# QKV product of a windowed attention kernel: two halves of 288 columns instead of 192 and 384, and the transposed v written beside the forward transform

## The chip, the cores and the metric

The kernel runs on one core of one Trainium2 chip. The metric is the device time of one execution in microseconds (us); lower is better. TensorE (PE) multiplies and loads weights, VectorE (DVE), ScalarE (ACT) and GpSimd (POOL) work element by element, and SyncE (SP) issues the DMAs.

## The reference

The input `x` has shape 8 x 192 x 128 x 128 in float32. Layer 0 normalises groups of channels, makes q, k and v with a 1x1 convolution, and works on windows of 8 x 8 tokens with 6 heads of 32 channels. The product of the Fourier transforms of q and k replaces q times k, and its inverse is the "o" that meets v:

```
qkv3 = wins.reshape(B_, N, 3, NH, HD).transpose(2, 0, 3, 1, 4)
o = jnp.fft.irfft2(jnp.fft.rfft2(qp) * jnp.fft.rfft2(kp), s=(PS, PS))
attn = jnp.einsum('bhnd,bhmd->bhnm', o, vv) + bias[None]
attn = jax.nn.softmax(attn, axis=-1)
y = jnp.einsum('bhnm,bhmd->bhnd', attn, vv)
x = x + (1x1 convolution of y)
```

Layer 1 normalises again, adds a Laplacian stencil and applies a 1x1 convolution (the "merge").

## The kernel before

A strip of 8 image rows holds 16 windows, so 8 pairs of windows (128 tokens each); there are 128 strips and 1024 pairs. The code is unrolled over iterations `it`. Each engine's instructions are written out by hand in one order, and `pair(lag)` is the pair on which an iteration works `lag` steps late. Eight iterations make a block; here "pair 0" to "pair 7" are the places in a block. Layer 1 follows 18 blocks behind: from then on iterations 0 to 5 of each block also hold a "piece", one 256-column part of the merge product. So the program has a head (statistics, tables), a first stage of 18 blocks without pieces, a second stage of 110 blocks with them, and a tail in which only pieces are left.

TensorE does in an iteration, in this order: transposes of the probabilities of pair n-4 (L418), a piece (L394 to L401), q, k and v of pair n (L456), two transposes of v (L460), the output projection of pair n-5 (L472 to L475), y of pair n-4 (L485), the inverse transform o of pair n-1 (L495), the forward transform of pair n (L505) and the scores of pair n-1 (L525). The QKV product is five products of split operands (high and low parts), accumulated. V's 192 columns go first, into their own bank, then Q's and K's 384 columns into the other bank of `b_q`.

The other engines follow on semaphores. ACT copies v out (`vs`, which raises `v_out`), takes the exponential of pair n-2 (L904), rounds q and k (`qkh`), copies the transposed v (`vT`, which raises `vT_out`), then y (`yT`), o (`osb`) and the transform of q (`qh`). All of these copies have line L859. DVE adds the position bias to the scores (L712), takes their maximum (L717), multiplies the transforms (`prod`, L721, which raises `prod_done`), does the stencil and statistics, then the remainder of q and k (`qkl`, L800, which raises `lo_out`), the residual (L808) and the sums (L818). POOL subtracts the maximum (L947), normalises (L936), and once in four pairs makes `xl` (L942). ACT also splits the input, once in four pairs, in three copies (`xhl`, `xh`, `xhb`) that stand just ahead of `vs` in its queue.

Three waits matter. The transposes wait for `v_out`; the QKV product waits for `vT_out` of the pair before; the forward transform waits for `lo_out`. The forward transform writes 384 of the 512 columns of each of the two banks of `b_t`, and DVE reads them for `prod` in the next iteration.

Of the kernel before, what the change touches and what calls it, by code (L numbers as in the profile page):

```python
# [13 lines left out]
C = 192  # L14
# [3 lines left out]
QK, QKV = 2 * C, 3 * C  # L18
# [72 lines left out]
def program(nc, x, out, w):  # L91
# [13 lines left out]
    with ExitStack() as ctx:  # L105
# [6 lines left out]
        def sem(name):  # L112
# [21 lines left out]
        vs, vT = sb("vs", [128, 5, C]), sb("vT", [128, 2, 2, 128])  # L134
# [26 lines left out]
        mw1, mb2 = late[0:2, at + 16:at + 16 + HID], late[0:1, at + 16 + HID:at + 16 + HID + N * NH]  # L161

        b_q, b_t, b_o, b_s = ps("b_q", 2), ps("b_t", 2), ps("b_o", 1), ps("b_s", 3)
        q_out, v_psum, vt_out = b_q[:, 0:QK], b_q[:, 512:512 + C], b_q[:, 512 + C:512 + C + 256]
        m_out = b_o[:, 192:512]
        b_r, scores, b_p = b_s[:, 0:256], b_s[:, 512 - C:512 + C], b_s[:, 1024:1024 + NH * N]
        y_at = (512 + C, 1024 + NH * N)
# [13 lines left out]
        v_mm, qkv_mm, t_mm, vT_mm, s_mm, pT_mm, y_mm, proj_mm, o_mm = map(sem, (  # L181
            "v_mm", "qkv_mm", "t_mm", "vT_mm", "s_mm", "pT_mm", "y_mm", "proj_mm", "o_mm"))
        lo_out, prod_done, s_out, max_done, sum_done, rec_done, x1_done = map(sem, (
            "lo_out", "prod_done", "s_out", "max_done", "sum_done", "rec_done", "x1_done"))
# [148 lines left out]
        def _(pe):  # L333
# [77 lines left out]
            for it, pair in pairs():  # L411
# [31 lines left out]
                if pair(0):  # L443
                    i, n = pair(0)
                    h, par = i // 4, i // NP % 2
                    if pair(1):
                        pe.wait_ge(vT_out, n - 1)
                    at = slice(i % 4 * 128, i % 4 * 128 + 128)
                    products = [(xh, wnh, 0), (xh, wnl, 0), (xhb, wnh, 1), (xl, wnh, 0), (xhl, wnl, 1)]
                    if i % 4 == 0:  # L450
                        pe.wait_ge(xh_done, 3 * (h + 1))
                        pe.wait_ge(xl_done, h + 1)
                        pe.wait_ge(xhl_done, h + 1)
                    for o, lo, up, done in ((v_psum, QK, QKV, v_mm), (q_out, 0, QK, qkv_mm)):
                        for k, (xx, ww, t) in enumerate(products):
                            last = mm(o, xx[:, h % 2, at], ww[:, par, t, lo:up], start=(k == 0), stop=(k == 4))  # L456
                        last.then_inc(done, 1)
                    pe.wait_ge(v_out, n)
                    for t in range(2):
                        last = nc.tensor.transpose(vt_out[:, t * 128:(t + 1) * 128],  # L460
                                                   vs[:, i % 5, t * N:t * N + 128], ident[:, :])
                    last.then_inc(vT_mm, 1)
                if pair(5):
# [35 lines left out]
                if pair(0):  # L499
                    i, n = pair(0)  # L500
                    pe.wait_ge(lo_out, n)
                    for k, (ff, xx) in enumerate(((fwdh, qkh), (fwdh, qkl), (fwdl, qkh))):
                        for win in range(2):
                            rows = slice(win * N, (win + 1) * N)
                            last = mm(b_t[0:NF, win * 512:win * 512 + QK], ff[rows, :], xx[rows, :],  # L505
                                      start=(k == 0), stop=(k == 2))
                    last.then_inc(t_mm, 1)
# [346 lines left out]
        def _(act):  # L854
# [3 lines left out]
            def copy(o, i):  # L858
                return A.activation(o, i, ACT.Copy)  # L859
# [15 lines left out]
            for it, pair in pairs():  # L875
# [29 lines left out]
                if pair(0):  # L905
                    i, n = pair(0)
                    act.wait_ge(qkv_mm, n)
                    copy(qkh[:, :], q_out).then_inc(hi_out, 1)
                    act.wait_ge(vT_mm, n)
                    copy(vT[:, i % 2, :, :].rearrange("p t m -> p (t m)"), vt_out).then_inc(vT_out, 1)  # L910
                if pair(4):
                    i, n = pair(4)
                    act.wait_ge(y_mm, n)
# [66 lines left out]
```

## Time and profile before

| | us |
|---|---|
| median of 3 runs | 6623.4 (6617.2 to 6633.11) |
| the profiled execution, its own time | 6616.41 |
| its span, first to last instruction | 6614.6 |
| PE busy, share of the span | 95% |
| DVE busy | 80% |
| ACT busy | 55% |
| POOL busy | 31% |
| mean granted TensorE clock | 0.978 of full speed |

Busy shares of TensorE count pipelined matmuls whose ends are modelled; the distance from one start to the next says more than the length of a row. An idle time in brackets stands in front of the instruction that ended it, with the instruction that released it.

### The profile page before, as it was taken

Reading aid. Unit: us, or ns where it says so; the run is one execution under the profiler, and the core shown is the slowest. Engines: PE = TensorE matmul, PEld = TensorE weight load, DVE = VectorE, ACT = ScalarE, POOL = GpSimd, SP = SyncE. Lnnn points to the kernel's source line nnn. Section 1 sums busy time; section 2 is a strip of 40 time slices with the busy share of each in tenths; the row PEclk is TensorE's granted clock in tenths of the full one; section 3 lists DMA queues with packets and bytes.
Section 4 is the critical chain, followed back from the end, with each engine's and each line's share of the span. In section 5 each row is a group of like instructions: output and inputs, shape, how many; then the busy total and the mean of one; then the engine's idle time right before and its main releaser. Section 6 shows DMA issues by size and latency. Waiting matters only on the chain.

```text
span 6614.6 us, 222120 instructions
## 1 busy us (share of the span) xinstructions
PE 6291.9 (95%) x95620; PEld 5340.6 (81%) x95620; DVE 5312.2 (80%) x11941; ACT 3664.4 (55%) x9024; POOL 2064.8 (31%) x2310
## 2 busy tenths in 40 slices
PE   7999999999999999999999999999999999999976
PEld 5888788888888888888888888888888888888844
DVE  5777788888888888888888888888888888888854
ACT  3666655555555555555555555555555555555500
POOL 1333333333333333333333333333333333333300
PEclk9999999999999999999999999999999999999966
DMA  3221133232332322322333223323223222232233
GB/s 128 66 66 40 56 93 90 84 84 82 89 104 71 97 82 83 104 70 81 98 90 96 72 82 92 101 77 91 82 83 104 77 78 70 64 85 64 69 99 92
DMA packets 378995, 551.42 MB, mean 83 GB/s; under 512 B 23398, under 2 KB 283561, under 8 KB 365738
## 3 DMA queue, kind: packets, MB, share of 16 engines
q1 hardware_dynamic: 378028, 537.21, 28.5%
q8 instruction: 768, 12.58, 0.8%
q14 instruction: 199, 1.63, 0.1%
HBM read 335.80 MB, written 201.33 MB: 81 GB/s over the span
## 4 chain that ended last, share of the span: by engine, by line
PE 58%; DVE 25%; POOL 9%; ACT 6%; issue 2%; SPq 0%; DMA 0%; DVEq 0%; ACTq 0%
PE b_q L456 13%; PE b_t L505 7%; POOL probs L947 5%; PE b_s L525 5%; PE b_s L418 4%; DVE qkl L800 4%; DVE bn L705 4%; PE b_o L495 4%; PE b_o L394 3%; DVE late L808 3%; PE b_o L396 3%; ACT probs L904 3%; DVE ssum L818 3%; PE b_s L485 3%; POOL xl L942 3%; DVE probs L712 2%
## 5 line engine op out<-in xcount | busy, mean ns | idle before, releaser
L936 POOL TENSOR_TENSOR probs<-probs,srec 128x384 f32<-128x384 f32 x1024 | 849.3, 829 | 3723.1 <-DVE srec L851 3723.1
L800 DVE TENSOR_TENSOR qkl<-b_q,qkh 128x384 fp32r<-128x384 f32 x1024 | 567.6, 554 | 634.9 <-ACT qkh L859 628.3
L947 POOL TENSOR_TENSOR probs<-probs,smax 128x384 f32<-128x384 f32 x1024 | 908.0, 887 | 413.8 <-DVE smax L717 413.8
L712 DVE TENSOR_TENSOR probs<-b_s,posb 128x384 f32<-128x384 f32 x1024 | 553.0, 540 | 331.2 <-PE b_s L525 330.6
L904 ACT ACTIVATE probs<-probs 128x384 f32<-128x384 f32 x1024 | 535.3, 523 | 479.8 <-POOL probs L947 479.1
L456 PE MATMUL b_q<-wnh,xh 128*128 128x192 f32 (+1 forms) x2048 | 791.7, 387 | 3.1 <-DVE xhl L822 2.7
L859 ACT ACTIVATE probsT<-b_s 128x384 f32<-128x384 f32 x1024 | 502.4, 491 | 501.3 <-PE b_s L418 501.3
L859 ACT ACTIVATE qh<-b_t 94x384 f32<-94x384 f32 x1024 | 498.4, 487 | 480.4 <-PE b_t L505 480.4
L525 PEld LDWEIGHTS b_s<-vT,osb 32*64 32x64 f32 x24576 | 450.6, 132 | 284.5 <-ACT osb L859 204.9
L859 ACT ACTIVATE yT<-b_s 128x256 f32<-128x256 f32 x1024 | 392.7, 384 | 460.3 <-PE b_s L485 458.2
L456 PE MATMUL b_q<-wnl,xh 128*128 128x192 f32 (+1 forms) x2048 | 632.5, 309 | 0.0
L808 DVE SCALAR_TENSOR_TENSOR late<-b_s,pb,xs 128x128 f32<-128x128 f32 (+1 forms) x2048 | 610.1, 339 | 27.2 <-PE b_s L475 5.2
L456 PE MATMUL b_q<-wnl,xhl 128*128 128x192 f32 (+1 forms) x2048 | 631.0, 308 | 0.0
L456 PE MATMUL b_q<-wnh,xhb 128*128 128x192 f32 (+1 forms) x2048 | 630.5, 308 | 0.0
L456 PE MATMUL b_q<-wnh,xl 128*128 128x192 f32 (+1 forms) x2048 | 629.6, 307 | 0.0
L859 ACT ACTIVATE vs<-b_q 128x192 f32<-128x192 f32 x1024 | 334.9, 327 | 518.6 <-PE b_q L456 512.9
L717 DVE TENSOR_REDUCE smax<-probs 128x6 f32<-128x384 f32 x1024 | 566.5, 553 | 35.5
L525 PE MATMUL b_s<-vT,osb 32*64 32x64 f32 x24576 | 592.4, 225 | 0.9 <-DVE late L808 0.7
L505 PE MATMUL b_t<-qkh,fwdh 64*94 64x384 f32 x2048 | 423.1, 410 | 171.0 <-DVE qkl L800 170.7
L495 PE MATMUL b_o<-inv_sb,prod 94*64 94x64 f32 x12288 | 582.9, 230 | 0.0
L418 PE MATMUL b_s<-ident_sb,probs 128*128 128x128 f32 x3072 | 561.3, 292 | 1.2 <-ACT yT L859 1.2
L721 DVE TENSOR_TENSOR prod<-qh,b_t 94x384 f32<-94x384 f32 x1024 | 553.5, 541 | 1.9 <-ACT qh L859 1.9
(143 smaller groups left out, 15231.2 us busy)
## 6 DMA issues: line engine op xcount, KB each, us to landing
ld<-in_x SPq DMA_DIRECT2D x96, 1024.0 KB, 4.9
late<-x_dram SPq DMA_DIRECT2D x112, 640.0 KB, 6.3
xs<-in_x SPq DMA_DIRECT2D x128, 512.0 KB, 5.7
x_dram<-late SPq DMA_DIRECT2D x128, 512.0 KB, 2.8
out<-late SPq DMA_DIRECT2D x128, 512.0 KB, 4.6
late<-x_dram SPq DMA_DIRECT2D x240, 192.0 KB, 6.7
xs<-in_x SPq DMA_DIRECT2D x128, 256.0 KB, 6.3
x_dram<-late SPq DMA_DIRECT2D x128, 256.0 KB, 3.6
```

The source lines that it names most:

```text
L418: last = nc.tensor.transpose(b_p[:, t * 128:(t + 1) * 128], probs[:, i % 3, 2 * t:2 * t + 2, :].rearrange("p w m -> p (w m)"), ident[:, :])
L456: last = mm(o, xx[:, h % 2, at], ww[:, par, t, lo:up], start=(k == 0), stop=(k == 4))
L495: last = mm(b_o[g * N:(g + 1) * N, k * N:(k + 1) * N], prod[:, g * 3 + k, :, :].rearrange("p h d -> p (h d)"), inv[:, :], start=True, stop ...
L505: last = mm(b_t[0:NF, win * 512:win * 512 + QK], ff[rows, :], xx[rows, :], start=(k == 0), stop=(k == 2))
L525: last = mm(scores[h * N:(h + 1) * N, s * N:(s + 1) * N], osb[r:r + HD, k, :], vT[r:r + HD, i % 2, int(t > g), win * N:(win + 1) * N], sta ...
L712: V.tensor_tensor(scored(i).rearrange("p (t w) m -> p t w m", w=2), scores.rearrange("p (t w m) -> p t w m", w=2, m=N), posb[:, :, :].unsq ...
L800: V.tensor_tensor(qkl[:, :], q_out, qkh[:, :].bitcast(F32), ALU.subtract).then_inc(lo_out, 1)
L808: last = V.scalar_tensor_tensor(out=x1s[0:m, t, u % 2, :].rearrange("p (r c) -> p r c", c=W)[:, :, col:col + 16], in0=b_r[0:m, t * 128:(t ...
L859: return A.activation(o, i, ACT.Copy)
L904: A.activation(pr, pr, ACT.Exp).then_inc(exp_done, 1)
L936: P.tensor_tensor(probs[:, i % 3, :, :], probs[:, i % 3, :, :], srec[:, i % 2, :].unsqueeze(2).broadcast_to([128, 6, N]), ALU.mult).then_i ...
L947: P.tensor_tensor(probs[:, i % 3, :, :], probs[:, i % 3, :, :], smax[:, i % 2, :].unsqueeze(2).broadcast_to([128, 6, N]), ALU.subtract).th ...
```

## The change

The ten matmuls of QKV stay ten, with 2880 columns in sum, but are cut at column 288 instead of 384. The half with the last 96 columns of K and all of V goes first and fills bank 1 of `b_q` from its start; the half with Q and the first 96 columns of K goes second and fills bank 0 up to its end. So Q and K still lie side by side, now across the banks' border. The transposed v is written to the last 128 columns of each bank of `b_t`. Two waits follow from this, and one goes.

```diff
-        q_out, v_psum, vt_out = b_q[:, 0:QK], b_q[:, 512:512 + C], b_q[:, 512 + C:512 + C + 256]
+        first = 512 - QKV // 2
+        q_out, v_psum = b_q[:, first:first + QK], b_q[:, first + QK:first + QKV]
+        vt_out = b_t.rearrange("p (t c) -> p t c", t=2)[:, :, QK:512]
...
-                    if pair(1):
-                        pe.wait_ge(vT_out, n - 1)
...
-                    for o, lo, up, done in ((v_psum, QK, QKV, v_mm), (q_out, 0, QK, qkv_mm)):
+                    for lo, up, done in ((QKV // 2, QKV, v_mm), (0, QKV // 2, qkv_mm)):
+                        o = b_q[:, first + lo:first + up]
...
                     pe.wait_ge(v_out, n)
+                    if pair(1):
+                        pe.wait_ge(prod_done, n - 1)
                     for t in range(2):
-                        last = nc.tensor.transpose(vt_out[:, t * 128:(t + 1) * 128],
+                        last = nc.tensor.transpose(vt_out[:, t, :],
...
                     pe.wait_ge(lo_out, n)
+                    pe.wait_ge(vT_out, n)
...
-                    copy(vT[:, i % 2, :, :].rearrange("p t m -> p (t m)"), vt_out).then_inc(vT_out, 1)
+                    copy(vT[:, i % 2, :, :], vt_out).then_inc(vT_out, 1)
```

The order of the instructions on TensorE at the start of a pair without a piece, before the change (`wnh`, `wnl` are the weights' high and low parts, `xh`, `xl`, `xhb`, `xhl` those of the input):

```order
L456 MATMUL b_q<-wnh,xh 128x192 [waits vT_out]
L456 MATMUL b_q<-wnl,xh 128x192
L456 MATMUL b_q<-wnh,xhb 128x192
L456 MATMUL b_q<-wnh,xl 128x192
L456 MATMUL b_q<-wnl,xhl 128x192
L456 MATMUL b_q<-wnh,xh 128x384
L456 MATMUL b_q<-wnl,xh 128x384
```

The same place on TensorE in the changed kernel:

```order
L457 MATMUL b_q<-wnh,xh 128x288
L457 MATMUL b_q<-wnl,xh 128x288
L457 MATMUL b_q<-wnh,xhb 128x288
L457 MATMUL b_q<-wnh,xl 128x288
L457 MATMUL b_q<-wnl,xhl 128x288
```

The five rows then come a second time for the other half. No instruction is added or taken away; the widths change and the first wait is gone.

From the transposes of v to the forward transform, TensorE before the change:

```order
L460 MATMUL b_q<-ident_sb,vs 128x128 [waits v_out]
L460 MATMUL b_q<-ident_sb,vs 128x128
L472 MATMUL b_s<-yT,wp 128x128 [waits s_out]
L473 MATMUL b_s<-yT,wp 128x128
L474 MATMUL b_s<-yT,wp 128x128
L475 MATMUL b_s<-yT,wp 128x128
L485 MATMUL b_s<-probsT,vs 32x64 [waits s_out,pT_out]
L485 MATMUL b_s<-probsT,vs 32x64 x11
L495 MATMUL b_o<-inv_sb,prod 64x64 [waits prod_done]
L495 MATMUL b_o<-inv_sb,prod 64x64 x5
L505 MATMUL b_t<-qkh,fwdh 94x384 [waits lo_out]
```

The same place in the changed kernel:

```order
L463 MATMUL b_t<-ident_sb,vs 128x128 [waits prod_done,v_out]
L463 MATMUL b_t<-ident_sb,vs 128x128
L475 MATMUL b_s<-yT,wp 128x128 [waits s_out]
L476 MATMUL b_s<-yT,wp 128x128
L477 MATMUL b_s<-yT,wp 128x128
L478 MATMUL b_s<-yT,wp 128x128
L488 MATMUL b_s<-probsT,vs 32x64 [waits s_out,pT_out]
L488 MATMUL b_s<-probsT,vs 32x64 x11
L498 MATMUL b_o<-inv_sb,prod 64x64 [waits prod_done]
L498 MATMUL b_o<-inv_sb,prod 64x64 x5
L509 MATMUL b_t<-qkh,fwdh 94x384 [waits vT_out,lo_out]
```

The wait for `prod_done` of the pair before has moved ahead of the projection and y, and the forward transform waits for two semaphores.

## Rows read from the trace of the kernel before

**Rows 1.** The page, busy time by engine.

```profile
PE 6291.9 (95%) x95620; PEld 5340.6 (81%) x95620; DVE 5312.2 (80%) x11941; ACT 3664.4 (55%) x9024; POOL 2064.8 (31%) x2310
```

**Rows 2.** Waits of TensorE (us in total, times, longest), second stage (902:6290).

```profile
PE b_t L505 <- DVE qkl L800: 133.7, 211, 1.6
```

**Rows 3.** Timeline (start us, us) of TensorE, pair 3 of one second-stage block.

```profile
2045.97 0.44 PE L456 MATMUL b_q<-wnh,xh 128*128 128x192 f32 x1
2046.25 0.28 PE L456 MATMUL b_q<-wnl,xh 128*128 128x192 f32 x1
...
2046.59 0.27 PE L456 MATMUL b_q<-wnl,xhl 128*128 128x192 f32 x1
2046.70 0.36 PE L456 MATMUL b_q<-wnh,xh 128*128 128x384 f32 x1
...
2047.42 0.34 PE L456 MATMUL b_q<-wnl,xhl 128*128 128x384 f32 x1
2047.59 0.38 PE L460 MATMUL b_q<-ident_sb,vs 128*128 128x128 f32 x2
...
2049.65 0.41 PE L505 MATMUL b_t<-qkh,fwdh 64*94 64x384 f32 x2
```

**Rows 4.** Timeline of DVE in the same pair.

```profile
2046.11 0.54 DVE L721 TENSOR_TENSOR prod<-qh,b_t 94x384 f32<-94x384 f32 x1
...
2048.31 0.56 DVE L800 TENSOR_TENSOR qkl<-b_q,qkh 128x384 fp32r<-128x384 f32 x1 [0.66 <-ACT qkh L859]
```

**Rows 5.** Timeline of TensorE where its granted clock is 0.5.

```profile
1626.61 0.41 PE L456 MATMUL b_q<-wnl,xh 128*128 128x192 f32 x1
...
1627.46 0.57 PE L456 MATMUL b_q<-wnh,xh 128*128 128x384 f32 x1
1627.84 0.52 PE L456 MATMUL b_q<-wnl,xh 128*128 128x384 f32 x1
...
1628.80 0.52 PE L456 MATMUL b_q<-wnl,xhl 128*128 128x384 f32 x1
```

**Rows 6.** Timeline of TensorE, the two instructions of one 288-column bias product.

```profile
745.00 0.51 PE L372 MATMUL b_o<-wn,negmean 128*128 128x288 f32 x1
...
745.34 0.41 PE L372 MATMUL b_o<-wn,negmean 128*128 128x288 f32 x1
```

**Rows 7.** Timeline of ACT in the pair of rows 3.

```profile
2046.90 0.33 ACT L859 ACTIVATE vs<-b_q 128x192 f32<-128x192 f32 x1 [0.91 <-PE b_q L456]
```

**Rows 8.** Timeline of TensorE and DVE, pair 0 of the same block.

```profile
2029.02 0.54 DVE L721 TENSOR_TENSOR prod<-qh,b_t 94x384 f32<-94x384 f32 x1
...
2029.27 0.38 PE L460 MATMUL b_q<-ident_sb,vs 128*128 128x128 f32 x2
...
2031.22 0.53 DVE L800 TENSOR_TENSOR qkl<-b_q,qkh 128x384 fp32r<-128x384 f32 x1
...
2031.81 0.41 PE L505 MATMUL b_t<-qkh,fwdh 64*94 64x384 f32 x2 [0.41 <-DVE qkl L800]
```

**Rows 9.** Timeline of DVE and TensorE, pair 7 of the same block.

```profile
2070.98 0.54 DVE L721 TENSOR_TENSOR prod<-qh,b_t 94x384 f32<-94x384 f32 x1
...
2071.46 0.38 PE L460 MATMUL b_q<-ident_sb,vs 128*128 128x128 f32 x2
```

**Rows 10.** Waits of the weight loader, first stage (98:902).

```profile
PEld b_q L460 <- ACT vs L859: 15.2, 68, 1.1
```

**Rows 11.** Timeline of TensorE and DVE, pair 0 of a first-stage block.

```profile
447.12 0.38 PE L460 MATMUL b_q<-ident_sb,vs 128*128 128x128 f32 x2
...
447.20 0.54 DVE L721 TENSOR_TENSOR prod<-qh,b_t 94x384 f32<-94x384 f32 x1
...
449.77 0.41 PE L505 MATMUL b_t<-qkh,fwdh 64*94 64x384 f32 x2 [0.53 <-DVE qkl L800]
```

**Rows 12.** Timeline of DVE and TensorE at the first pair, where three semaphores are waited for.

```profile
97.33 0.69 DVE L822 TENSOR_TENSOR xhl<-xs,xhl 64x512 fp32r<-64x512 f32 x1
...
98.16 0.50 PE L456 MATMUL b_q<-wnh,xh 128*128 128x192 f32 x1 [2.72 <-DVE xhl L822]
```

## The prediction

> **What bounds the kernel now.** I read the page first: TensorE is busy for 95% of the span, the weight loader for 81%, DVE for 80% [rows 1]. That says who is nearest to full, not who ends a wait, so the waits of the second stage come next, since it holds 880 of the 1024 pairs (110 blocks of eight). There the forward transform waits for `qkl` in 211 pairs, 133.7 us in sum [rows 2], about two pairs in a block. The timelines show which. In pair 0 TensorE stands still for 0.41 us before the forward transform, which starts 0.06 us after the end of `qkl` (2031.22 + 0.53 = 2031.75) [rows 8]; pair 6 is the other. In pair 3, `qkl` ends at 2048.87 and the forward transform starts at 2049.65 [rows 3, 4]: DVE is 0.78 us early and TensorE sets the time. So pairs 1 to 5 are TensorE's, and what it saves there shortens the kernel; in pairs 0, 6 and 7 a chain through DVE, POOL and ACT sets it, and a saving of TensorE turns into waiting.
>
> That gives a count. 880 less 211 are 669 pairs without the wait. One in each block, pair 7, I take off: its `prod` ends at 2070.98 + 0.54 = 2071.52, later than its transposes start (2071.46) [rows 9], and the change makes them wait for it. Left are 559, five in a block.
>
> **The ten matmuls.** In pair 3 the first matmul of V starts at 2045.97 and the second at 2046.25; that first step belongs to the piece ahead and stays. From 2046.25 the starts are (2046.70 - 2046.25) / 4 = 0.1125 us apart with 192 columns. From 2046.70 to the transposes at 2047.59 are 0.89 us for five of 384 columns, 0.173 each and some 0.02 on the first. Together 1.34 us from the second matmul to the transposes [rows 3].
>
> Now per column: 384 columns at 2.4 per ns are 0.160, so 0.173 is the stream and 0.013 more. But 192 columns would be 0.080 and take 0.1125. Something else bounds them. The stretch at half clock (granted 0.5, the 1.2 GHz level) says what: (1627.46 - 1626.61) / 4 = 0.2125 with 192 columns, (1628.80 - 1627.84) / 3 = 0.320 with 384 [rows 5]. 0.320 is 384 columns at 1.2 per ns exactly; 0.2125 is what 255 columns would take, and so is 0.1125 at full clock but for 5 ns. So a 192-column matmul costs as much as 256, a floor that I put down to the load of 128 fp32 weights under it. Half of V's issue is empty. With 288 columns the stream is above the floor.
>
> The price of 288 columns isn't in the trace for this form. Nearest is the bias product: its two instructions pass 288 columns twice each, and end at 745.51 and 745.75 [rows 6], 0.24 us for 576 columns, 0.120 for 288. From below that is 0.120, nothing on top. From the row of 384, with the same 0.013 on top, it is 0.133. A straight line between 0.1125 and 0.173 gives 0.143. At worst it costs what 384 do, 0.173, if widths were rounded up. Rows 6 exclude rounding for the bias form, so I take 0.133: nine steps and 0.02 are 1.22 us instead of 1.34, a saving of 0.12 a pair.
>
> TensorE: Matmul & The Clock Gate, section Back-to-back issue gap, in the Trainium skill, gives a spacing of N/2.4 + 2.5 ns at full clock, which is 0.1225 us for 288 columns (an estimate from that page). The trace disagrees at both widths that it has (0.083 against 0.1125, 0.1625 against 0.173), so the sum doesn't use it; with it the matmuls alone would save 1.34 - 1.12 = 0.22 a pair.
>
> **The copy of v.** It can start only when the first half is done, and that is now 96 columns longer. Before, the copy starts at 2046.90, 0.04 after V's last matmul ends (2046.59 + 0.27), and ends at 2047.23; the transposes' weights are loaded from about 2047.42 [rows 3, 7]. After: V's half has its last start at 2046.25 + 3 x 0.133 = 2046.65; it lasts some 0.31 (between 0.27 and 0.34), so the copy runs from 2047.00 to 2047.33, and the load may begin 0.05 to 0.10 later, at 2047.38 to 2047.43. Unhindered it would begin at about 2047.34. So the wait for `v_out`, which has 0.19 us to spare now, is at its edge. The load has some slack against the stream before it; I take 0.01 as lost, 0.11 as the saving. This also caps it: at 0.120 a matmul the copy ends only at 2047.29, so no more than some 0.18 to 0.20 can be won in a pair.
>
> 559 x 0.11 = 61 us.
>
> **The wait for `prod_done` ahead of the transposes.** The transposes now go to the banks that `prod` is read from. Behind them on TensorE are projection, y, o and the forward transform; ACT waits for y and o. In pair 3 `prod` ends at 2046.65, 0.94 before the transposes [rows 3, 4]: free. In pair 0 it ends at 2029.56, and they start at 2029.27 [rows 8]. The hold-up is 0.29, about 0.06 for the release, and some 0.05 because their weights can't be loaded ahead: 0.40. This goes into the 0.41 of idle time before the forward transform in the same pair, since `qkl` is set by a chain that doesn't contain the transposes. Cost nothing, with nothing to spare. In pair 7 the hold-up is 0.16; the next forward transform that matters, pair 0's, is set by DVE, which is busy without a break from pair 7 into pair 0, so it is hidden too. In the first stage pair 0 (and pair 4 alike) has `prod` ending at 447.74 against a start of 447.12 [rows 11]: 0.62 + 0.11 = 0.73 held up, and 0.53 of idle time, which by the starts of o and the transform is nearer 0.58. So 0.15 is lost twice a block, 18 x 2 x 0.15 = 5 us. The same stage gains nothing, for in half its pairs the transposes already wait for `vs` (68 of 144 [rows 10]), held by a copy of the input ahead of it on ACT, and in others the wait for `qkl` ends last.
>
> **Two waits on one instruction.** Where the trace has one wait before a matmul it starts 0.06 after the release [rows 8]; with three it starts 0.14 after (97.33 + 0.69 = 98.02, start 98.16) [rows 12]. So a second wait costs between 0 and 0.08 where the semaphore that comes last is checked first; `lo_out` is written first. I take 0.05, in pair 0 of 110 blocks (in pair 6 DVE hides it) and in some three pairs of the 18 first blocks: 8 us. The wait for `vT_out` itself is free: the copy `vT` ends before `qkl` does. The dropped wait cost nothing, and copies, bytes and DMAs stay as they are.
>
> **Sum.** -61 + 5 + 8 = -48 us, so 6616.4 becomes 6568. The median of the runs shown is 7 us above the profiled time, hence 6575.
>
> **The rivals.**
> *The copy's cap is reached.* 288 columns at 0.120 to 0.1225: 0.19 x 559 = 106 saved, less 13: -93, 6530. For it: the bias rows. Against: no fp32r row of full clock runs without the extra. 0.12.
> *Interpolated price, 0.143.* The pair saves 1.34 - 1.31 = 0.03: -17 + 13 = -4 us, 6619, no change. For it: if the floor of the weight load and the stream add up partly. 0.11.
> *Rounded up: 288 cost what 384 do.* 9 x 0.173 + 0.02 = 1.58, 0.24 more in 559 pairs: +134, with the 13 above and some 20 in the first stage near 6790. Against it are rows 6 and the linear 0.320. It decides from 0.146 a matmul. 0.06.
> *The hold-ups aren't hidden.* If `qkl` or POOL's and ACT's chain moves with the held transposes, 0.40 + 0.16 a block in 110 blocks and 0.73 twice in 18 are 62 + 26 = 88 instead of 5: +35 us, 6658, slower. Point of decision: more than about 0.45 of the 0.56 per block showing. For it: ACT copies y and o, both now late, ahead of the next block's work; against: `qh` follows the forward transform, later still. 0.08.
>
> **How the numbers follow.** My forecast, a gain of 20 to 75 us with 0.11 a pair as its middle, has 0.63. A measurement of this kernel tells from no change about 0.2%, 13 us. Faster by more: 0.63 + 0.12 and 0.01 of the interpolated case, 0.76; within: 0.10; slower: 0.06 + 0.08 = 0.14. The range takes in the first rival and the interpolated price, and leaves out the slower cases: 6528 to 6620.
>
> **What would show it.** Pair 3 after: starts of the ten matmuls 0.133 apart (0.120, 0.143 or 0.173 name the rival), transposes 0.11 to 0.12 earlier after the second matmul, `vs` starting 0.10 later. Block length in the second stage shorter by 0.5 to 0.55 us. Pair 0: transposes some 0.05 after `prod`, idle time before the forward transform near 0, its start still 0.06 to 0.11 after `qkl`. Waits of the forward transform for `qkl` fewer or shorter; first stage longer by 5 to 10 us. The prediction is wrong if the price of 288 is off by more than 0.01, or if pairs 1 to 5 begin to wait for `vs` or `qkl`.

## The result and the profile after

| kernel | median us | lowest to highest | runs |
|---|---|---|---|
| before | 6626.27 | 6617.2 to 6633.11 | 4 |
| after | 6564.04 | 6561.89 to 6579.31 | 4 |

The ratio is 0.9912, its 95% interval 0.9895 to 0.9928: the change makes the kernel 58 us faster, by its middle. The profiled execution took 6561.89 us. The page of the kernel after, its head and the busy times, answers to [rows 1]:

```profile
span 6560.1 us, 223912 instructions
PE 6223.4 (95%) x95620; PEld 5256.2 (80%) x95620; DVE 5294.0 (81%) x11941; ACT 3630.8 (55%) x9024; POOL 2064.4 (31%) x2310
```

TensorE is as full as before, on a span 54.5 us shorter than the 6614.6 of before. Where that came from is read by stage. I cut the span at the starts of the first QKV matmul of pair 0, of pair 144 (where the pieces begin) and of the last pair. Windows of the kernel after, then the second stage of the kernel before; behind the stretch stand its length, the five busy times with their counts, the granted clock, the DMA share and GB/s:

```profile
98.00:906.90 808.90, 755.68 (x12682) 627.14 (x12683) 581.08 (x1353) 498.76 (x1257) 285.51 (x319) 1.00 0.19 57
906.90:6234.90 5328.00, 5171.34 (x81574) 4441.75 (x81572) 4491.10 (x10147) 3106.99 (x7725) 1771.13 (x1977) 1.00 0.30 85
6234.90:6560.00 325.10, 230.85 (x803) 145.54 (x801) 176.27 (x355) 9.35 (x21) 5.80 (x7) 0.66 0.35 95
```

```profile
904.10:6289.70 5385.60, 5232.48 (x81574) 4512.28 (x81572) 4509.87 (x10148) 3146.29 (x7724) 1771.56 (x1977) 1.00 0.30 84
```

The second stage went from 5385.6 to 5328.0 us, 57.6 less; the first from 805.9 to 808.9, 3.0 more; head and tail are as before. So all of the gain is in the second stage. Its pairs, as the median distance from one pair's first QKV matmul to the next pair's:

| pair of a block | 0 | 1 | 2 | 3 | 4 | 5 | 6 | 7 |
|---|---|---|---|---|---|---|---|---|
| before, us | 6.438 | 5.957 | 5.957 | 6.375 | 6.375 | 5.176 | 6.050 | 5.872 |
| after, us | 6.236 | 5.840 | 5.844 | 6.259 | 6.277 | 5.082 | 6.040 | 6.075 |

Pairs 1 to 5 each gained 0.09 to 0.12, 0.54 in all, and 0.54 x 110 blocks is 59 us. Pair 7 lost 0.20 and pair 0 won the same 0.20 back. This is the pattern to explain; pair 3 after on TensorE, to be laid beside [rows 3] (start, duration):

```profile
2036.34 0.48 PE L457 MATMUL b_q<-wnh,xh 128*128 128x288 f32 x1
2036.66 0.30 PE L457 MATMUL b_q<-wnl,xh 128*128 128x288 f32 x1
2036.80 0.29 PE L457 MATMUL b_q<-wnh,xhb 128*128 128x288 f32 x1
...
2037.72 0.29 PE L457 MATMUL b_q<-wnl,xhl 128*128 128x288 f32 x1
2037.85 0.38 PE L463 MATMUL b_t<-ident_sb,vs 128*128 128x128 f32 x2
2039.91 0.41 PE L509 MATMUL b_t<-qkh,fwdh 64*94 64x384 f32 x2
```

From the second matmul to the transposes are 1.19 us in nine steps, 0.132 each, where 1.34 were needed. The first step became longer, 0.32 instead of 0.28. Together the ten take 1.51 us where they took 1.62. ACT's copy of v in the same pair, which answers to [rows 7]:

```profile
2037.39 0.33 ACT L863 ACTIVATE vs<-b_q 128x192 f32<-128x192 f32 x1 [1.03 <-PE b_q L457]
```

It ends at 2037.72, 0.13 before the transposes start. Before, it ended 0.36 ahead of them. Now pair 0, TensorE and then DVE, beside [rows 8]:

```profile
2018.44 0.48 PE L457 MATMUL b_q<-wnh,xh 128*128 128x288 f32 x1
...
2019.82 0.29 PE L457 MATMUL b_q<-wnl,xhl 128*128 128x288 f32 x1
2020.32 0.41 PE L463 MATMUL b_t<-ident_sb,vs 128*128 128x128 f32 x2 [0.20 <-DVE prod L725]
...
2022.42 0.41 PE L509 MATMUL b_t<-qkh,fwdh 64*94 64x384 f32 x2
```

```profile
2019.63 0.54 DVE L725 TENSOR_TENSOR prod<-qh,b_t 94x384 f32<-94x384 f32 x1
...
2021.83 0.53 DVE L804 TENSOR_TENSOR qkl<-b_q,qkh 128x384 fp32r<-128x384 f32 x1
```

`prod` ends at 2020.17 and the transposes start 0.15 later. Pair 7 of the same block, beside [rows 9], shows the same distance (2061.03 + 0.54 = 2061.57, start 2061.72):

```profile
2061.72 0.41 PE L463 MATMUL b_t<-ident_sb,vs 128*128 128x128 f32 x2 [0.16 <-DVE prod L725]
```

```profile
2061.03 0.54 DVE L725 TENSOR_TENSOR prod<-qh,b_t 94x384 f32<-94x384 f32 x1
```

In pairs 1 to 5 the transposes start 0.13 after the last QKV matmul started; in pair 0 it is 0.49 and in pair 7 0.45 (medians of the stage). So they are held up by 0.36 and 0.32, which is about what these two pairs have to give: 0.11 each, saved by the matmuls, and the 0.41 of idle time in front of pair 0's forward transform. That still starts 0.06 after `qkl` (2022.36), now without idle time before it. The waits of TensorE say the same for all blocks of the second stage (total us, times, longest), beside [rows 2]:

```profile
PE b_t L509 <- DVE qkl L804: 99.5, 128, 1.7
PE b_t L463 <- DVE prod L725: 33.0, 165, 0.8
```

The forward transform waits in 128 pairs for 99.5 us instead of in 211 for 133.7, and a new wait of 33.0 us stands at the transposes. The sum has hardly moved.

### The profile page after: what moved, and what is told of

It reads as the page before. It is cut to its first block, busy times and chain, and to the rows that moved or that the text cites. A ratio compares the mean times of both kernels' runs of the same rounds, so it can differ in the third digit from the quotient of the medians.

```text
span 6560.1 us, 223912 instructions
## 1 busy us (share of the span) xinstructions
PE 6223.4 (95%) x95620; PEld 5256.2 (80%) x95620; DVE 5294.0 (81%) x11941; ACT 3630.8 (55%) x9024; POOL 2064.4 (31%) x2310
## 4 chain that ended last, share of the span: by engine, by line
PE 61%; DVE 23%; POOL 9%; ACT 5%; issue 2%; SPq 0%; DMA 0%; DVEq 0%; ACTq 0%
PE b_q L457 12%; PE b_t L509 7%; PE b_s L529 5%; POOL probs L951 5%; PE b_o L498 4%; PE b_s L420 4%; DVE bn L709 4%; PE b_s L488 3%; PE b_o L396 3%; DVE late L812 3%; PE b_o L398 3%; DVE qkl L804 3%; DVE ssum L822 3%; PE b_t L463 3%; POOL xl L946 3%; ACT probs L908 2%
## 5 line engine op out<-in xcount | busy, mean ns | idle before, releaser
L457 PE MATMUL b_q<-wnh,xh 128*128 128x288 f32 x2048 | 762.2, 372 | 2.8 <-DVE xhl L826 2.7
L457 PE MATMUL b_q<-wnh,xl 128*128 128x288 f32 x2048 | 606.8, 296 | 0.0
L457 PE MATMUL b_q<-wnl,xhl 128*128 128x288 f32 x2048 | 606.0, 296 | 0.0
L457 PE MATMUL b_q<-wnh,xhb 128*128 128x288 f32 x2048 | 605.6, 296 | 0.0
L457 PE MATMUL b_q<-wnl,xh 128*128 128x288 f32 x2048 | 605.5, 296 | 0.0
L822 DVE TENSOR_REDUCE ssum<-probs 128x6 f32<-128x384 f32 x1024 | 546.2, 533 | 0.0
```

Source lines behind the costliest of these rows:

```text
L822: V.tensor_reduce(ssum[:, i % 2, :], scored(i), AX.X, ALU.add).then_inc(sum_done, 1)
```

## The experiments

Eleven more runs follow, one of them of the kernel after again; the experiments are described in groups, not in the order in which they ran. Each ratio is to runs of the kernel before on the same chip.

| run | median us | ratio, 95% interval | first stage us | second stage us |
|---|---|---|---|---|
| after | 6564.04 | 0.9912, 0.9895 to 0.9928 | 808.9 | 5328.0 |
| waits and place alone | 6638.99 | 1.0028, 1.0018 to 1.0037 | 807.9 | 5390.3 |
| 256 then 320 | 6570.96 | 0.9928, 0.9915 to 0.994 | 807.6 | 5328.6 |
| transposes behind projection | 6528.76 | 0.9861, 0.9846 to 0.9876 | 803.4 | 5302.7 |
| 224 then 352 | 6594.73 | 0.996, 0.9948 to 0.9973 | 810.0 | 5351.7 |
| POOL's `xl` later | 6582.58 | 0.9945, 0.9933 to 0.9956 | 792.9 | 5353.2 |
| both of these moves | 6558.0 | 0.991, 0.9897 to 0.9923 | 779.2 | 5346.9 |
| waits swapped (one run) | 6596.23 | | 809.9 | 5351.0 |
| before, `xl` later | 6617.83 | 0.9992, 0.9983 to 1.0001 | 788.9 | 5397.6 |
| `xl` later only where free | 6521.22 | 0.9843, 0.9829 to 0.9858 | 778.7 | 5301.7 |
| the kernel after, again | 6574.04 | 0.9927, 0.9914 to 0.9941 | 810.3 | 5326.2 |
| `xl` where free, widths 192 and 384 | 6581.96 | 0.9939, 0.9925 to 0.9952 | 783.6 | 5364.6 |

The kernel after, run again, repeats its ratio within the two intervals, and its stages within 2 us. The stage lengths are the finer measure, since executions of one kernel differ by up to 29 us, which I put down to the tail (last section). The edits below are against the kernel after, unless another is named.

My theory was: the gain is the price of a matmul of 288 columns against those of 192 and 384, and the hold-ups by the new wait go into time in which TensorE stood idle. The rivals: the gain is in the moved transposes, or the waits cost something that the widths pay for.

### The place and the waits without the widths

```diff
-        first = 512 - QKV // 2
-        q_out, v_psum = b_q[:, first:first + QK], b_q[:, first + QK:first + QKV]
+        q_out, v_psum = b_q[:, 0:QK], b_q[:, 512:512 + C]
...
-                    for lo, up, done in ((QKV // 2, QKV, v_mm), (0, QKV // 2, qkv_mm)):
-                        o = b_q[:, first + lo:first + up]
+                    for o, lo, up, done in ((v_psum, QK, QKV, v_mm), (q_out, 0, QK, qkv_mm)):
```

> This kernel keeps the old widths (192 and 384) and takes only the new place of the transposed v with its waits. My theory: the hold-ups at the transposes are hidden in the second stage (pair 7 by pair 0's idle time, pair 0 by its own 0.4 us), and show only in the first stage, about 0.2 us in pairs 0 and 4 of 18 blocks. So 3 to 12 us slower than before, middle 8. The rival, that the hold-ups aren't hidden, wants 0.6 us a block in 110 blocks more: over 50 us slower. A third view, that the new place itself saves something (the dropped wait), wants it faster than before.

Measured: 1.0028 (1.0018 to 1.0037), some 18 us by its middle; the profiled span is 6621.2, 6.6 more than before, and the stages have 2.0 and 4.7 of it. Against the kernel after the second stage is 62.3 us longer. So the whole gain is that of the widths. The new place and its waits cost 7 us by the stages, inside the 3 to 12 that I had given, and 12 to 24 by the interval, outside of it. Part of the latter goes with the clock of its executions, which took 6623 and 6627 us at a mean granted clock of 0.979 and 6645 and 6646 at 0.974; at 0.979 the kernel before took 6615 to 6618. In this kernel, too, pair 0 is 0.20 shorter than before (6.240) and pair 7 0.20 longer (6.077), and pairs 1 to 5 are as before within 0.02: the shift between these two comes with the new place and its waits, not with the widths. In the usual block the two together take 12.31 us in either kernel, but of the 109 such sums 30 lie under 12.2 before, 12 here and 6 in the kernel after. Their mean is 12.345 before, 12.385 here and 12.363 after. The 0.04 is 4.4 us in 110 blocks, nearly all of the 4.7 that the stage lost. So the hold-ups are hidden in the usual block and cost 2 to 4 us over the stage.

### Other widths: 256 then 320, and 224 then 352

```diff
-        first = 512 - QKV // 2
+        cut = 320
+        first = 512 - cut
...
-                    for lo, up, done in ((QKV // 2, QKV, v_mm), (0, QKV // 2, qkv_mm)):
+                    for lo, up, done in ((cut, QKV, v_mm), (0, cut, qkv_mm)):
```

The second of them has `cut = 352`.

> The changed kernel with its cut moved: 256 columns first (V and 64 of K), then 320. Theory of a floor at 256 columns and stream plus 0.013 us above it: 256 cost 0.1125 us and 320 cost 0.146, so from the second matmul to the transposes 4 x 0.1125 + 0.02 + 5 x 0.146 = 1.20 us against 1.23 with 288 and 288; 10 to 17 us faster than the changed kernel, 70 to 80 faster than before. Rival, a price that rises in a straight line between 192 and 384 columns: 256 cost 0.133, 320 cost 0.153, 1.32 us, 40 to 50 us slower than the changed kernel. If instead the copy of v was what limits the changed kernel, its earlier start here would gain 0.05 us a pair and more, 30 us faster than the changed kernel.

> The changed kernel with the cut moved further: 224 columns first (V and 32 of K), then 352. Floor theory: 224 cost the same 0.1125 us as 192 and 256, and 352 cost 0.160, so 4 x 0.1125 + 0.02 + 5 x 0.160 = 1.27 us against 1.23: 15 to 25 us slower than the changed kernel, and 40 faster than before. Straight-line rival: 224 cost 0.123 and 352 cost 0.163, 1.33 us, the time of e1. Rounding-up rival (multiples of 128): 224 as 256 and 352 as 384, the same as with 192 and 384, the time of e1.

TensorE in pair 3 with 256 and 320 columns:

```profile
2036.12 0.47 PE L458 MATMUL b_q<-wnh,xh 128*128 128x256 f32 x1
2036.43 0.28 PE L458 MATMUL b_q<-wnl,xh 128*128 128x256 f32 x1
...
2036.90 0.31 PE L458 MATMUL b_q<-wnh,xh 128*128 128x320 f32 x1
...
2037.63 0.38 PE L464 MATMUL b_t<-ident_sb,vs 128*128 128x128 f32 x2
```

and with 224 and 352:

```profile
2036.77 0.45 PE L458 MATMUL b_q<-wnh,xh 128*128 128x224 f32 x1
2037.06 0.27 PE L458 MATMUL b_q<-wnl,xh 128*128 128x224 f32 x1
...
2037.51 0.33 PE L458 MATMUL b_q<-wnh,xh 128*128 128x352 f32 x1
...
2038.31 0.38 PE L464 MATMUL b_t<-ident_sb,vs 128*128 128x128 f32 x2
```

With the kernels before and after this gives a table of prices at full clock: the distance of two starts of one width, and the first step, from the first matmul behind a piece to the second.

| columns | 192 | 224 | 256 | 288 | 320 | 352 | 384 |
|---|---|---|---|---|---|---|---|
| a matmul, us | 0.112 | 0.111 | 0.117 | 0.132 | 0.147 | 0.160 | 0.173 |
| columns / 2.4 per ns | 0.080 | 0.093 | 0.107 | 0.120 | 0.133 | 0.147 | 0.160 |
| first step | 0.277 | 0.291 | 0.305 | 0.319 | | | |

From 288 columns up, the price is the stream and 0.012 to 0.014 more. Below 256 it is 0.111 to 0.112 whatever the width, and the transposes and the projection, which pass 128 columns, step by 0.11 too (2037.85 to 2038.07 for two in the kernel after). That this floor is the load of the 128 weight columns, as the prediction had it, is argued: no run changed the weights. The trace of the kernel after disagrees with the Trainium skill (TensorE: Matmul & The Clock Gate, Back-to-back issue gap), whose N/2.4 + 2.5 ns would be 0.1225 for 288 columns (an estimate from that page); 0.132 was measured. The page calls its formula the gap of an isolated matmul, which counts too little for narrow ones, because the weight load isn't in it, and too much for wide ones. The rows agree on the narrow side (0.112 against an estimated 0.0825 at 192 columns) and not on the wide one (0.173 against an estimated 0.1625 at 384).

With 224 the second stage is 23.7 us longer than after, within the 15 to 25 that the floor gave: the V half wins only 0.021 a matmul against 288 columns, and the other half loses 0.028. It is 24 us faster than before by the medians, where I had given 40. For 256 and 320 I had given a gain of 10 to 17 us, and there is none: 5328.6 against 5328.0. The forecast missed because 256 columns cost 0.117 and not the floor's 0.1125, so the five plus five cost 1.32, as ten of 288 do. From the first matmul to the transposes are 1.51 us with either (2037.63 - 2036.12; 2037.85 - 2036.34), 1.54 with 224, 1.62 with 192. The halves could thus be shifted by 32 columns at no price, and the optimum is flat.

### The order of the two waits

```diff
                     pe.wait_ge(vT_out, n)
-                    pe.wait_ge(lo_out, n)
...
+                    pe.wait_ge(lo_out, n)
...
                     if pair(1):
                         pe.wait_ge(prod_done, n - 1)
+                    pe.wait_ge(v_out, n)
```

Here the wait for `vT_out` comes ahead of that for `lo_out`, and the one for `prod_done` ahead of that for `v_out`.

> The changed kernel with the two waits of the transposes and the two of the forward transform written in the other order. Theory: the wait written first is held by the matmul itself (0.05 us from release to start), the second by an instruction of its own ahead of it (0.14). So the transposes now start 0.05 after prod in pairs 0 and 7 instead of 0.14, and the forward transform 0.14 after qkl where it waits for it, instead of 0.05. Rival (my prediction's): the wait written first is the dear one, so the changed kernel pays already at the forward transform, and it gets cheaper here. In time under 10 us either way.

It lost more than the 10 us that I had given at most: the second stage is 23 us longer than in the kernel after. It was one run, so I read it by its rows. Pair 0, TensorE, then DVE:

```profile
2027.54 0.44 PE L463 MATMUL b_t<-ident_sb,vs 128*128 128x128 f32 x2 [0.17 <-DVE prod L725]
...
2029.82 0.41 PE L509 MATMUL b_t<-qkh,fwdh 64*94 64x384 f32 x2
```

```profile
2026.94 0.54 DVE L725 TENSOR_TENSOR prod<-qh,b_t 94x384 f32<-94x384 f32 x1
...
2029.14 0.53 DVE L804 TENSOR_TENSOR qkl<-b_q,qkh 128x384 fp32r<-128x384 f32 x1
```

`prod` ends at 2027.48 and the transposes start 0.06 later; `qkl` ends at 2029.67 and the transform starts 0.15 later. In the kernel after it is the other way round, 0.15 and 0.06. So of two waits the one written first is the cheap one when it comes last, and the one written second costs 0.09 more when it comes last. The medians of pair 0 over the stage are the same 0.06 and 0.15. The trace shows what the second wait is, an instruction of its own on the weight loader's sequencer, at the line of `pe.wait_ge(prod_done, ...)` (the view of L461 in the kernel after, around this pair):

```profile
L461 PEldq EVENT_SEMAPHORE  x1: 51/51/51, 2020.2 to 2020.2; - x1
```

It takes 0.05 us and stands there once a pair (1023 times). In pairs 0 and 7 it starts 0.04 after the end of `prod`, and the transposes start 0.11 after its start. With the waits swapped, the instruction of this line waits for `v_out`. In pairs 1 to 5 the transposes now pay for `v_out` written second: their lengths grow by 0.03 to 0.05 each. In pair 3, 0.035 of the 0.046 has been lost by the start of the projection (medians). So the copy of v is near its edge, as the prediction had it. The kernel after has its waits in the better order.

### The transposes behind the projection

```diff
-                    pe.wait_ge(v_out, n)
-                    if pair(1):
-                        pe.wait_ge(prod_done, n - 1)
-                    for t in range(2):
-                        last = nc.tensor.transpose(vt_out[:, t, :],
-                                                   vs[:, i % 5, t * N:t * N + 128], ident[:, :])
-                    last.then_inc(vT_mm, 1)
...
                     mm(b_r[:, 128:256], wp[:, 1, CA:256], yb, start=False, stop=True).then_inc(proj_mm, 1)
+                if pair(0):
+                    i, n = pair(0)
+                    pe.wait_ge(v_out, n)
+                    if pair(1):
+                        pe.wait_ge(prod_done, n - 1)
+                    for t in range(2):
+                        last = nc.tensor.transpose(vt_out[:, t, :],
+                                                   vs[:, i % 5, t * N:t * N + 128], ident[:, :])
+                    last.then_inc(vT_mm, 1)
```

> The changed kernel with the transposes of v moved behind the output projection on TensorE, so that 0.9 us of other work stands ahead of their two waits. Theory (hold-ups are hidden in the second stage and show in the first): the second stage moves little, 0 to 5 us, and the first stage gets back its 0.2 us in pairs 0 and 4 and the waits for the copy of v in pairs 1, 3 and 5, some 0.1 each: 8 to 18 us faster than the changed kernel. Rival, that the hold-ups of pairs 0 and 7 cost in the second stage too: 30 to 60 us faster. Rival on the other side: ACT's copy of the transposed v comes 0.9 us later and pushes the copies of y and o behind it, which would make it slower than the changed kernel by 0.1 us and more a pair, over 50 us.

This takes the cause of the hold-up away without taking a wait away. Pairs 0 and 7 went back to 6.444 and 5.873, the lengths before. In the usual block their sum is the same, so the hold-ups are hidden there, shown from the other side; the mean of the sum fell from 12.363 to 12.323, 4.4 us in the stage. Yet the stage is 25.3 us shorter, where I had given 0 to 5. The total, 34 us less than after by the ratios, is what the rival of hold-ups that aren't hidden would have given, but most of it lies elsewhere: in pair 6, 5.860 instead of 6.040, 17 us of the 25.3 by the means of that pair. POOL of the kernel after around the start of pair 6 (first matmul at 2053.96):

```profile
2053.60 0.83 POOL L940 TENSOR_TENSOR probs<-probs,srec 128x384 f32<-128x384 f32 x1 [4.03 <-DVE srec L855]
2054.39 1.28 POOL L946 TENSOR_TENSOR xl<-xs,xh 128x512 fp32r<-128x512 f32 x1
2055.63 1.28 POOL L951 TENSOR_TENSOR probs<-probs,smax 128x384 f32<-128x384 f32 x1
```

and with the transposes behind the projection (first matmul at 2043.83):

```profile
2043.28 0.83 POOL L942 TENSOR_TENSOR probs<-probs,srec 128x384 f32<-128x384 f32 x1 [3.83 <-DVE srec L857]
2044.07 1.30 POOL L948 TENSOR_TENSOR xl<-xs,xh 128x512 fp32r<-128x512 f32 x1
2045.32 1.28 POOL L953 TENSOR_TENSOR probs<-probs,smax 128x384 f32<-128x384 f32 x1
```

The last of the three begins 1.67 after the pair's first matmul in the one, 1.49 in the other. The projection is done 0.22 earlier, with it DVE's residual and `srec`, and then, 0.18 to 0.19 earlier, POOL's normalisation, `xl` and the subtraction, for which the exponential and the transposes of the probabilities wait. In the first stage four pairs of a block (0, 1, 4 and 5) are 0.21 shorter and two (2 and 6) 0.21 longer, and 5.5 us of it are won in all, where I had given 8 to 18.

### POOL's remainder of x behind the subtraction

```diff
-                h = (it + 4) // 4
-                if it % 4 == 2 and 0 <= h < PAIRS // 4:
-                    pool.wait_ge(xh_done, 3 * h + 2)
-                    P.tensor_tensor(tokens(xl, 0, h), windows(0, h), tokens(xh, 0, h).bitcast(F32), ALU.subtract
-                                    ).then_inc(xl_done, 1)
...
                                     ALU.subtract).then_inc(sub_done, 1)
+                h = (it + 4) // 4
+                if it % 4 == 2 and 0 <= h < PAIRS // 4:
+                    pool.wait_ge(xh_done, 3 * h + 2)
+                    P.tensor_tensor(tokens(xl, 0, h), windows(0, h), tokens(xh, 0, h).bitcast(F32), ALU.subtract
+                                    ).then_inc(xl_done, 1)
```

The rows above put 1.28 us of `xl` ahead of the subtraction, in pairs 2 and 6. I moved it behind, in three kernels: after, after with the late transposes, and before.

> The changed kernel with one step of POOL's order changed: the low part of the input (xl, 1.28 us, in pairs 2 and 6) comes behind the subtraction of the maximum instead of ahead of it. My theory of the 34 us that the later transposes won beyond the changed kernel: pair 6 of the second stage waits for a chain in which POOL makes xl first, and that chain began earlier because the projection, and with it DVE's residual, sums and reciprocal, came earlier. Then this kernel takes most of the 0.86 us of idle time out of pair 6, 0.4 to 0.8 us a block in 110 blocks: 45 to 90 us faster than the changed kernel. Rival, pair 6 is bound by DVE's own work: under 10 us.

> Both: xl behind the subtraction, and the transposes of v behind the projection. If pair 6 was POOL's, the later transposes can no longer win there (their 0.18 us a block), but the hold-ups for the product in pairs 0 and 7 and in the first stage have less idle time to hide in once xl is out of the way, so taking them out should now win 0.1 to 0.4 us a block: 10 to 50 us faster than e5, and the fastest of all. Rival: the two gains simply add, 34 us over e5, with pair 6 shorter by another 0.18 us.

> The kernel before, with xl behind the subtraction. If the idle time of pair 6 has nothing to do with the change of this study, this wins the same 45 to 90 us over before that e5 wins over the changed kernel. If the changed kernel's saving is in pairs 1 to 5 alone, e5 stays 50 to 75 us faster than this; if the change's hold-ups lose their cover, less, 30 to 50.

The theory that this was worth 45 to 90 us fell, and so did the forecast that both moves together would be the fastest of all. The first stage gained 16 us on the kernel after, 24 with the late transposes, 17 on the kernel before; the second lost 25, 44 and 12 against the same kernels without it. In the first stage of the kernel after, pair 6 went from 5.913 to 5.179 and pair 2 from 5.454 to 5.177. In the second, pair 6 is shorter (5.809), but pair 2 is 0.43 longer (6.274), and its DVE shows why, with POOL and TensorE below:

```profile
2020.31 0.68 DVE L678 SCALAR_TENSOR_TENSOR late<-late 128x512 f32<-128x512 f32 x1
2020.92 1.90 DVE L662 TENSOR_TENSOR dg<-late 128x645 f32<-128x645 f32 x1
2022.74 0.55 DVE L804 TENSOR_TENSOR qkl<-b_q,qkh 128x384 fp32r<-128x384 f32 x1
```

```profile
2019.62 0.83 POOL L946 TENSOR_TENSOR probs<-probs,smax 128x384 f32<-128x384 f32 x1 [1.11 <-DVE smax L721]
2020.41 1.72 POOL L952 TENSOR_TENSOR xl<-xs,xh 128x512 fp32r<-128x512 f32 x1
```

```profile
2023.34 0.42 PE L509 MATMUL b_t<-qkh,fwdh 64*94 64x384 f32 x2 [0.37 <-DVE qkl L804]
```

`xl` now lies beside the stencil's sum `dg`, which takes 1.90 us instead of 0.82, and takes 1.72 itself instead of 1.28; `qkl` is queued behind `dg`, and the forward transform waits for it. The rows agree with the Trainium skill (SBUF — State Buffer, Who interferes with whom), by which a DVE instruction with two inputs in SBUF contends with a GpSimd instruction that reads SBUF. Over the stage, DVE's busy time rose by 94 us on the same work and POOL's by 81.

These kernels also try the count of pairs. With `xl` late in both, the second stage is 44.4 us shorter after than before (5353.2 against 5397.6), and not 57.6: pair 2, now set by DVE, gains 0.013, while pairs 1, 3, 4 and 5 gain 0.42 in sum as ever.

### The moves together, and the widths once more

Where the stencil doesn't run beside it, `xl` may go late: in the first stage, and in pair 6. The kernel has this edit on top of the transposes behind the projection:

```diff
+            def behind(it):
+                return it < 8 * STENCIL_LAG or it % 8 == 6
...
-                if it % 4 == 2 and 0 <= h < PAIRS // 4:
+                if it % 4 == 2 and not behind(it) and 0 <= h < PAIRS // 4:
...
                                     ALU.subtract).then_inc(sub_done, 1)
+                if it % 4 == 2 and behind(it) and 0 <= h < PAIRS // 4:
```

> The changed kernel with the transposes of v behind the projection (as in e3) and xl behind the subtraction of the maximum only where DVE does no long operation from SBUF to SBUF beside it: everywhere before the stencil starts, and in pair 6, not in pair 2. Theory from the traces of e3, e5 and e6: POOL and DVE slow each other when both run such operations, xl against the 128x645 sum of the stencil in pair 2 (0.82 us grew to 1.90), so leaving pair 2 alone keeps e3's second stage and adds some 0.04 us a block in pair 6, and the first stage gets e6's 779 us instead of e3's 803: 25 to 33 us faster than e3, near 6500. Rival, that e6's first stage owed its time to something else than the order of xl: the time of e3, 6528.

> The changed kernel once more, beside the others on one chip: 50 to 65 us faster than before at the same mean granted clock.

> The kernel of e9 with the old widths, 192 columns for V and 384 for Q and K. If the saving of the equal halves is one of TensorE's issue, in pairs where TensorE sets the time, it is lost here whole, and in the first stage too, where the transposes no longer hold anything: 60 to 80 us slower than e9. Rival, that part of the saving came through the copies and waits around the transposes: under 50 us slower.

The kernel with both moves has stages of 778.7 and 5301.7 us and the best time of all, 6521.22, ratio 0.9843 (0.9829 to 0.9858). I had given near 6500, 25 to 33 us less than with the late transposes alone. The stages have 25.7 of it, the ratios 12, and its tail is the longest of all (last section). Its windows, first and second stage and the tail:

```profile
98.00:876.70 778.70, 741.79 (x12684) 627.45 (x12684) 580.65 (x1352) 497.64 (x1257) 286.63 (x319) 0.99 0.20 59
876.70:6178.40 5301.70, 5125.27 (x81574) 4400.15 (x81572) 4439.37 (x10149) 3137.51 (x7724) 1812.30 (x1977) 1.00 0.31 86
6178.40:6522.00 343.60, 249.68 (x802) 156.23 (x800) 176.39 (x354) 9.22 (x21) 5.81 (x7) 0.59 0.34 89
```

Nearly all that it gained on the kernel with late transposes alone is in the first stage (24.7 us). In the second (5301.7 against 5302.7) pair 6 became 0.047 shorter, which would be 5 us; the stage shows 1.0. With the old widths the same kernel has 5364.6: the widths are worth 62.9 us there and 4.9 in the first stage, and the ratios differ by 0.96%, some 64 us, inside the 60 to 80 that I had given. So the gain of the widths doesn't depend on where the transposes and their waits stand: 62.3 beside the kernel after, 62.9 here. It does depend on how many pairs TensorE sets, as the kernels with `xl` late in pair 2 show.

## Why the prediction was right

- **Which pairs count.** 559 pairs at 0.11 were to give 61 us. Pairs 1 to 5 gained 0.117, 0.113, 0.116, 0.098 and 0.094, 59 us in 110 blocks. That TensorE sets the time of these five and of no other was right. Against waits and place alone it is the widths' 62 us. Pair 7 was left out of the count because of the new wait; in the two last kernels that wait holds nothing up there, and it still gains nothing (5.866 against 5.868). Its forward transform starts 0.06 after `qkl` in the kernel before too, so DVE sets that pair anyway, which the prediction didn't see.
- **The price of 288 columns.** 0.133 was taken, 0.132 measured; the rivals' 0.120, 0.143 and 0.173 are out. The 0.120 came from rows 6, read as two passes of 288 columns in one instruction; no row shows the passes. The two parts from which it came, the stream plus 0.013 and a floor for the narrow ones, hold at 224, 320 and 352 columns too. At 256 the floor of 255 columns gave 0.1125 and 0.117 was measured.
- **The first step "belongs to the piece ahead and stays".** This was wrong by 0.04: it grows with the width of the first matmul, 0.277 to 0.319. The 0.02 on the first matmul of the wide half went away with the change of width, which I had kept, and I had taken off 0.01 for the copy of v. 1.34 - 1.19 = 0.15, less 0.04, is the 0.11 that the ten matmuls won. The right size came out of three small errors that cancel.
- **The copy of v.** It was to start 0.10 later and be at its edge. After the second matmul it starts at 0.73 (2037.39 - 2036.66) where it started at 0.65 [rows 3, 7]; with the waits swapped, the 0.09 of the second wait cost 0.03 to 0.05 a pair, so about 0.05 of slack was left (an estimate from that one run).
- **The wait for `prod_done`.** In the usual block of the second stage the hold-ups are hidden, as said: pair 7 loses 0.20 and pair 0 wins 0.20. Their sizes were wrong. I measured them from the old starts of the transposes, but the ten matmuls end 0.11 earlier now, and the start comes 0.15 after `prod` and not the 0.05 that I named. So pair 7 is held up by 0.32 and not 0.16, pair 0 by 0.36 against 0.40. The idle time of pair 0 and the matmuls' saving in the two pairs were just enough, and not in every block: 2 to 4 us of the stage went there, which I had put at nothing.
- **The first stage.** 5 us were to be lost. The stage lost 3.0 and, in the second run of the kernel after, 4.4. The mechanism is there: pairs 0 and 4 are 0.21 longer (5.672 to 5.880, 5.666 to 5.881), where 0.15 was given, though not in all of the 18 blocks, and lost 6.0 us in sum. Pair 5 won 2.9 back, in three of the last blocks; why, I don't know.
- **The second wait on an instruction.** Its 8 us at the forward transform are the term whose mechanism failed. The transform starts 0.06 after `qkl` as before, since `lo_out` is written first. The price exists, 0.09, but at the wait for `prod_done`, where idle time covers it in the usual block.

Sum by the stages: -57.6 + 3.0, with under 0.2 in head and tail, make -54.5, against the predicted -48. The kernel with waits and place alone splits the -57.6 into -62.3 for the widths, against -61, and +4.7 for the place and its waits, where the second wait was to cost 0.05 in each of 110 blocks, 5.5. That these two nearly agree is luck: the 4.7 are hold-ups that aren't hidden in some blocks. The rest of the difference is the first stage, +3.0 where 5 and, by the second wait, 2.7 were to be lost. The time that I gave, 6575, is 11 above the median measured.

## What to carry to other kernels

Measure the distance between starts for two widths before splitting a product: when the narrow part sits on the floor, even widths above it are free speed, and the optimum is flat around them. When TensorE must wait for two things, write first the one that comes last. And before moving work on GpSimd out of a chain, see what VectorE does in its new place: a free engine can still slow its neighbour.

## What the runs showed of the hardware that I hadn't expected

- VectorE and GpSimd slow each other: `dg` 0.82 to 1.90 us and `xl` 1.28 to 1.72 side by side. The kernel after has a mild case in pair 6, where the subtraction takes 1.28 instead of 0.83.
- The second of two waits costs 0.09 us more than the first when it ends last (0.15 against 0.06); it is an instruction of 0.05 us of its own.
- The first QKV matmul behind a piece delays the second by more than its own price, and by 0.014 more for each 32 columns (0.277, 0.291, 0.305, 0.319), about the stream of 32 columns. In pairs 6 and 7, which have no piece, it grows likewise, from 0.17 with 192 columns to 0.22 with 288. What the rest of the delay is stays open.
- Executions of one kernel differ by up to 29 us with the mean granted clock: before took 6607.19 at 0.981 and 6636.51 at 0.975 on one chip. The stages are at 0.99 to 1.00 in every profile, so I put it down to the tail, where TensorE is partly idle and for part of the time at the lower of its levels, 1.2 GHz: 325.1 us at a granted 0.66 after, 343.6 at 0.59 in the best kernel, with the same 802 or 803 matmul records. The tails of all thirteen profiles go the same way, from 322.8 us at 0.66 to 344.2 at 0.59 between the last pair's first matmul and the end. No kernel has a profile of a short and of a long execution, so this stays an inference. The best kernel's profiled execution shows 19 us less of gain over before than its stages. What sends the clock down there I didn't test.
